# One multiplication moved ahead of four small operations in a mixture-of-experts tile loop

## The reference, cut to what matters

```python
def _L1_ffn_ref(x, router_w, router_bias, gate_w, up_w, down_w, sgate_w, sup_w, sdown_w):
    flat = x.reshape(B * T, D)                                   # 2048 x 256
    scores = softmax(flat @ router_w.T + router_bias)            # 32 experts
    topk_scores, topk_idx = top_k(scores, 4)
    topk_scores = topk_scores / clip(topk_scores.sum(-1), 1e-12)
    h = silu(einsum('nd,ehd->neh', flat, gate_w)) * einsum('nd,ehd->neh', flat, up_w)
    expert_out = einsum('neh,edh->ned', h, down_w)
    out = (take_along_axis(expert_out, topk_idx) * topk_scores).sum(1)
    return out + silu(flat @ sgate_w.T) * (flat @ sup_w.T) @ sdown_w.T
```

## Time and profile before

| | us |
|---|---|
| median of 3 runs | 2196.73 |
| lowest and highest run | 2196.61, 2201.77 |
| the profiled execution, its own time | 2206.42 |
| its span, first to last instruction | 2204.6 |
| TensorE busy | 1987.3 (90%) |
| VectorE busy | 1452.5 (66%) |
| ScalarE busy | 1103.5 (50%) |
| GpSimd busy | 744.6 (34%) |
| granted TensorE clock, mean | 0.981 of full |

### The profile page before, as it was taken

How to read it: one execution, slowest core, us unless ns; L and a number is a source line. 1 busy time by engine, 2 the same in 40 slices (tenths; PEclk the granted TensorE clock), 3 DMA queues, 4 the chain that set the end, 5 groups by cost and what they waited for, 6 DMA issues and landing times.

```text
span 2204.6 us, 35748 instructions
## 1 busy us (share of the span) xinstructions
PE 1987.3 (90%) x12400; PEld 1331.5 (60%) x12400; DVE 1452.5 (66%) x4611; ACT 1103.5 (50%) x2793; POOL 744.6 (34%) x767
## 2 busy tenths in 40 slices
PE   7888988998999999888899999878888898999889
PEld 4555556776565564565546778556665466666746
DVE  7665546555575557787732876699787775767753
ACT  4333333756433332587711565678687323778322
POOL 3222134100222232235532565566353432011253
PEclk9999999999999999999999999999999999999999
DMA  8999701100100002101142445400140100000100
GB/s 284 334 332 349 258 5 53 59 20 1 63 1 1 1 1 93 40 21 62 48 197 91 141 146 149 163 1 1 60 146 13 39 1 15 2 2 1 42 1 38
DMA packets 40449, 180.55 MB, mean 82 GB/s; under 512 B 6832, under 2 KB 24496, under 8 KB 37136
## 3 DMA queue, kind: packets, MB, share of 16 engines
q1 hardware_dynamic: 32640, 157.17, 20.9%
q0 software_dynamic: 7632, 21.11, 2.7%
HBM read 155.06 MB, written 98.89 MB: 115 GB/s over the span
## 4 chain that ended last, share of the span: by engine, by line
PE 60%; DVE 22%; ACT 9%; issue 4%; POOL 4%; DMA 1%; POOLq 0%; DVEq 0%; another core or an unknown queue 0%; SPq 0%; ACTq 0%
PE ps L248 40%; PE ps L814 4%; ACT BIG L898 3%; PE ps L799 3%; PE ps L2121 3%; DVE BIG L858 3%; ACT BIG L348 2%; PE ps L833 2%; DVE XN L305 2%; PE ps L2133 1%; PE ps L322 1%; PE ps L316 1%; DVE SML L289 1%; PE ps L3603 1%; DVE SML L2947 1%
## 5 line engine op out<-in xcount | busy, mean ns | idle before, releaser
L248 PE MATMUL ps<-BIG 128*128 128x256 f16 (+2 forms) x1616 | 327.5, 352 | 15.0 <-DVE BIG L2749 5.6
L898 ACT ACTIVATE BIG<-BIG,SML 128x256 f32<-128x256 f32 (+1 forms) x768 | 315.2, 482 | 23.3 <-DVE SML L858 23.2
L248 PEld LDWEIGHTS ps<-BIG 128*128 128x128 f16 (+1 forms) x1616 | 216.4, 135 | 106.4 <-issue 64.8
L348 ACT ACTIVATE BIG<-ps 128x512 f32<-128x512 f32 (+1 forms) x336 | 175.7, 560 | 149.4 <-PE ps L814 133.7
L814 PE MATMUL ps<-CST,BIG 128*128 128x128 f32 x1408 | 210.8, 283 | 41.1 <-ACT BIG L898 25.6
L706 POOL TENSOR_TENSOR BIG<-BIG 128x512 f16<-128x512 f32 x120 | 141.6, 1182 | 266.2 <-ACT BIG L640 235.6
L814 PEld LDWEIGHTS ps<-CST,BIG 128*128 128x128 f32 x1408 | 156.2, 143 | 113.5 <-issue 61.2
L248 PE MATMUL ps<-XN,BIG 128*128 128x512 f16 x864 | 195.5, 380 | 10.2 <-ACT BIG L617 6.0
L858 DVE CUSTOM_DVE_ANT_0 BIG<-ps,BIG 128x256 f32<-128x256 f32 x512 | 181.0, 419 | 32.0 <-PE ps L799 31.1
L252 POOL TENSOR_SCALAR SML<-SML 128x4 f32<-128x4 f32 (+1 forms) x92 | 24.4, 266 | 456.6 <-DVE SML L292 187.8
L248 PE MATMUL ps<-WA,XT 128*128 128x256 f32 (+2 forms) x576 | 135.2, 375 | 24.4 <-DVE X L2293 6.4
(11 more groups left out here) (418 smaller groups left out, 3894.2 us busy)
## 6 DMA issues: line engine op xcount, KB each, us to landing
slots<-in_zeros SPq DMA_DIRECT2D x28, 2640.0 KB, 67.1
WA<-slots SPq DMA_DIRECT2D x95, 132.0 KB
BIG<-in_l1e SPq DMA_DIRECT2D x2, 4224.0 KB
BIG<-spread SPq DMA_DIRECT2D x16, 512.0 KB, 6.3
BIG<-in_l0e SPq DMA_DIRECT2D x8, 768.0 KB, 8.4
BIG<-in_ctxT SPq DMA_DIRECT2D x8, 512.0 KB, 6.6
BIG<-in_ctxT SPq DMA_DIRECT2D x16, 256.0 KB, 3.0
BIG<-in_ctx SPq DMA_DIRECT2D x16, 256.0 KB, 3.5
```

What stands on the lines that cost most here:

```text
L248: m = T.e.matmul(ps, l, r, start=i == 0, stop=i == len(pairs) - 1)
L348: return q.e.activation(o, i, ACT.Copy) if q is A else q.e.tensor_copy(o, i)
L898: A.e.activation(s[:, q, 0:kn[q]], s[:, q, 0:kn[q]], ACT.Exp, bias=mx[:, q:q + 1], scale=-1.0, accum_out=c["SUM"][b % 2][:, at_sum:at_sum ...
```

## The change

In VectorE's loop the multiplication of tile j-1 is now written ahead of the four small operations of tile j. The copy and the background step stay behind both. No operation is added, removed or altered, and the other engines' instructions are the same.

```diff
             for j in range(TILES + 3):
+                if 1 <= j <= TILES:
+                    waits(V, ("gu", j - 1), ("sg", j - 1))
+                    if j >= 4:
+                        waits(V, ("hxt", j - 4))
+                    V.e.tensor_tensor(c["HX"][(j - 1) % 3], c["SG"][(j - 1) % 3], bank("gu", j - 1)[:, P:2 * P],
+                                      ALU.mult).then_inc(*V.sig("hx", j - 1))
                 if j < TILES:
                     waits(V, (f"xg{j % 5}", j))
                     if j >= 8:
@@ -2241,12 +2247,6 @@
                     V.e.tensor_reduce(to, eq, AX.X, ALU.add).then_inc(*V.step())
                     V.wait_ge(*V.last())
                     V.e.tensor_scalar(c["toi"][j % 8].bitcast(I32), to, spill, None, ALU.add).then_inc(*V.sig("dsti", j))
-                if 1 <= j <= TILES:
-                    waits(V, ("gu", j - 1), ("sg", j - 1))
-                    if j >= 4:
-                        waits(V, ("hxt", j - 4))
-                    V.e.tensor_tensor(c["HX"][(j - 1) % 3], c["SG"][(j - 1) % 3], bank("gu", j - 1)[:, P:2 * P],
-                                      ALU.mult).then_inc(*V.sig("hx", j - 1))
                 if j >= 3 and j % 2:
                     tile_out(V, c, j - 3)
```

## The result

The changed kernel is slower, by a little: a median of 2207.56 us (2198.08 to 2212.14, 22 runs) against 2200.74 (2194.27 to 2208.37, 22 runs) for the one before on the same chip. The ratio is 1.0028, 95% interval 1.0016 to 1.0040, so 3.5 to 8.8 us. No change was forecast, with a range up to 2204.

The account below looks back on a forecast made before the run. TensorE was taken to hold 60% of the chain, VectorE's lateness costing at most 7.7 us in the loop. All terms were 0 except 0.5 us for seams; added to the median of 2196.7 this gave 2197.2 us, range 2190 to 2204.

Parts of the forecast that it names:

- The multiplication: H in VectorE's tile turn: moved ahead of the small operations, it comes at the same time; cost and gain 0.
- Sooner: Rival: the multiplication frees TensorE sooner at the entry of three late stretches, 2.5 us, so 2194.2; chance 0.06.
- The seams: Starts between successive VectorE operations: new ones as short as old (0.13 behind a small operation); estimate 0.5 us.
- The rival by which the seams cost 6.0 us: New VectorE seams start only after the operation before ends, 0.24 us a tile over 25 tiles, so 2202.7; chance 0.07.
- The small operations and the loads: S, VectorE's four operations on tile targets, end 1.2 to 1.6 us later; SP's loads keep about 2 us cover; cost 0.
- The copy C: VectorE's copy of a finished tile in odd turns comes about 0.83 us later; bank and scatter absorb it; cost 0.
- GpSimd becomes late: Rival: 48 scatters lengthen from 0.96 to 1.86, 43 us, under GpSimd's 89 idle; time stays 2197; no chance given.
- The cap of 7.7 us: Most that VectorE's lateness costs in the tile loop, matched with TensorE's waits for the multiplication; said to cap any gain.
- The chances: For the whole run's measured time: 0.90 for no change, 0.05 for faster, 0.05 for slower.

Follow-up runs that it names:

- e3: The changed kernel with the copy put back ahead of the small operations, right behind the multiplication: loop 168.27 us.
- e1: The kernel before, order kept, with tile loads also waiting for the gate and up product of the tile five before: loop 168.33 us.
- e4: The changed kernel without the 95 scatters, their area filled early instead: loop 165.13 us.
- e5: The kernel before without the 95 scatters, their area filled early instead: loop 165.10 us.
- after: The changed kernel in the first comparison: median 2207.56 us, loop 172.79 us.
- e6: The changed kernel with every scatter held until the targets of the tile three on are there, so later and evenly spaced: ratio 0.9995 to the kernel before.
- before: The kernel before the change, in the first comparison: median 2200.74 us, loop 167.53 us.
- before_again: The kernel before, unaltered, profiled a second time, on chip 11: loop 167.4 us, longest turn 2.74 us.
- after_again: The changed kernel run once more, unaltered, on chip 4: loop 172.12 us.
- e2: The changed kernel with the four small operations done one tile further ahead, so that loads come early: loop 3.3 us over the kernel before.
- e12: The changed kernel with each load also waiting for ScalarE's copy of the transposes of the tile four before: median 2205.97 us, on chip 0.
- e10: The kernel before with loads held for gate-and-up matmuls five tiles back and scatters for those three on: median 2201.20 us, loop 166.47.
- e11: The kernel before with only the scatters held for the gate-and-up matmuls three tiles on: median 2200.58 us, loop 166.45.
- e9: The kernel before with every scatter held until the targets four tiles on are there: ratio 1.0012, loop 166.67 us.
- e13: The changed kernel with TensorE's registers loaded ten at a time in every tenth turn instead of five in every fifth: median 2198.64 us.
- e16: The kernel before with the background quantization put behind the loop: 87.87 us of loop behind turn 42.
- e14: The kernel before with TensorE's registers loaded ten at a time in every tenth turn: median 2198.53 us, ratio 1.0025.

## Why the prediction was wrong

- **The multiplication: right.** e3 has it in front, with the copy right behind it, and a loop of 168.27 where e1 with the old order and equally late loads has 168.33; e4 and e5 have it in either place with 165.13 and 165.10. "Sooner" was not seen.
- **The seams: right in length, 0 rather than 0.5 us in effect where there are no scatters.** 0.13 and 1.13 stand where forecast, and turns 0 to 19 take 35.22 and 35.21 us in e4 and e5. What the +0.44 of turns 0 to 19 in after is, no run shows. The rival by which the seams cost 6.0 us gave nearly the right total, 6 to 7 us, by a mechanism that did not happen. The prediction set the 0.13 against the Trainium skill, "VectorE: DVE Perf Modes", The DRAIN you can't avoid; that section goes on to say that a next operation that is not held starts earlier, so the two agree.
- **The small operations and the loads: nearly right.** Priced at 0; e1 shows 0.8 us of loop.
- **The copy C: this step failed.** It said that GpSimd's scatter "starts later in every second tile" and that GpSimd, 89.3 us idle, "takes that up. Cost: 0", and the rival "GpSimd becomes late" ended in "the time stays 2197". GpSimd did take it up: a scatter takes 1030 ns in the mean in both kernels. But the copy's place is not free: with S between it and H the loop takes 172.79 and 172.12 us, with it back right behind H (e3) 168.27, against 167.53 before. The time is lost in a few turns in which TensorE's signals come up to 2.15 us late. I looked for harm on the engines that wait for GpSimd, and it came on TensorE's signals, which don't. Whether the copy does this through the moment of its scatter or otherwise stays open.
- **The cap of 7.7 us was no cap.** It was read from L2128's wait for the multiplication. That wait rose to 15.8 us in after and 13.6 in e6, whose loop is shorter than that of before and of before_again. Only the interval between turns says what a wait costs.
- **The chances: too sure.** 0.90 for no change rested on a list in which a transfer that starts later could cost time only by landing late.

What is shown, each by one profile a run on chips of the first kind: the loss comes with S between H and the copy (after, after_again, e2, e12 with 170.8 to 172.8 us; before, e1, e3, e10, e11 with 166.5 to 168.3), and on chip 0 the medians agree (2205.97 us in e12, 2201.20 and 2200.58 in e10 and e11); it sits in turns with held signals; late loads alone (e1) and late, evenly spaced scatters in the order of before (e10, e11) don't bring it; and loads moved away from the scatters around turn 45 don't cure it (e12). What is not shown is that the loss needs the scatters, their pairs, the register loads or the background work. The runs meant for that (e4 to e9, e13 to e16) were on chips where nothing in the loop is held, whatever the order. Open too is whether the changed kernel is slower on those chips: its altered forms there are level with their controls without scatters and 1.0 to 1.1 us of loop over them with scatters. And what holds the signals is open: that something is shared between the scatters' traffic and TensorE's way of raising a semaphore is a guess from times alone. The traces with held signals are also those that lack increments; whether the tracing has a part in it, no run shows.

No variant beats the kernel before: e6 is at 0.9995 and e10 and e11 at 0.9997, all with intervals across 1.

## What to carry to other kernels

When a reordering leaves the critical engine's work as it was, list also which DMA issues change their distance to each other, and don't price them at nothing because the issuing engine has idle time. Compare the length of turns, not the sum of waits or one span: six turns held the loss, and the spans were equal. Before a variant is said to cure a loss, run the unaltered slow kernel beside it on the same chip. Here the kernel before alone was repeated on each chip, and most of the variants ran where the loss may never have been.

## What the runs showed of the hardware

- A semaphore increment of TensorE could arrive up to 2.15 us after the modelled end of its matmul, and several came at once (1288.56 to 1288.68). ScalarE and VectorE then sit idle while TensorE's own records look busy.
- Chips differ in this. The traces of the first comparison and of chips 0 and 4 have 3 to 26 such increments in the loop and 20 to 30 outside it, in the kernel before too; those of chips 9, 10 and 11 have none in the loop. The kernel before is 7.6 to 8.9 us slower on the first kind (2200.5 to 2200.8 against 2191.9 to 2192.9).
- TensorE's register loads grew out of proportion. On chips of the second kind, with five at a time, turns 50 and 70 take 2.03 and 2.23 us (before_again), with ten at a time 3.46 each (e14), over a plain turn of 1.63. That is 0.4 to 0.6 against 1.8 us, and the loop was 4.6 us longer for half as many loads.
- On the same kind the 95 scatters cost 2.3 us of loop at an engine that was idle half the time (before_again against e5); in the new order, evenly spaced and later, 1.1 us (e6 against e4).
